# Scaling of the output gates moved from GpSimd to ScalarE, head by head, in a gated delta-rule block

## What is computed

```python
o = gated_delta_rule(q, k, v, g, beta)          # 32 heads, DK = 48, DV = 96
gate = (h @ Wg).reshape(b, t, H, DV)
o = rmsnorm(o, gnorm_w) * jax.nn.silu(gate)
o = o.reshape(b, t, VD) @ Wo
```

## Time and profile before

| | |
|---|---|
| time, median of 3 runs | 2520.83 us |
| lowest, highest | 2520.28, 2522.46 us |
| profiled execution, its own time | 2518.24 us |
| its span, first to last instruction | 2516.3 us |
| mean granted clock of TensorE | 0.978 of 2.4 GHz |
| busy: TensorE, VectorE | 2352.5 us (93%), 2004.9 us (80%) |
| busy: ScalarE, GpSimd | 1407.4 us (56%), 1279.2 us (51%) |

### The profile page before, as it was taken

One profiled execution on the slowest core, in us unless ns is written; L12 is line 12 of the kernel. 1 busy time (PEld: TensorE's weight loads), 2 busy tenths in 40 slices (PEclk: granted clock), 3 DMA queues, 4 the chain that ended last, 5 costly groups with the idle time before them and its releaser, 6 DMA issues. The chain is left out here.

```text
span 2516.3 us, 53535 instructions
## 1 busy us (share of the span) xinstructions
PE 2352.5 (93%) x18800; PEld 1889.7 (75%) x18800; DVE 2004.9 (80%) x4146; ACT 1407.4 (56%) x3331; POOL 1279.2 (51%) x2046
## 2 busy tenths in 40 slices
PE   6599999999999999999999999999999998699997
PEld 2378888888888888888888888888888887546665
DVE  5678888888888888888888888888888887235544
ACT  3256666666666666666666666666666665322221
POOL 3456566666666666666666666656566665100000
PEclk9689999999999999999999999999999999799998
DMA  4211121112111211121112111211121110221100
GB/s 129 69 36 35 27 61 34 34 33 55 35 36 36 54 37 35 36 54 36 36 36 55 36 36 36 55 36 36 36 55 36 36 26 9 66 62 34 34 9 9
DMA packets 203849, 103.20 MB, mean 41 GB/s; under 512 B 97009, under 2 KB 185018, under 8 KB 203586
## 3 DMA queue, kind: packets, MB, share of 16 engines
q1 hardware_dynamic: 203266, 99.65, 17.0%
q10 hardware_dynamic: 320, 0.13, 0.0%
HBM read 69.89 MB, written 2.54 MB: 29 GB/s over the span
## 5 line engine op out<-in xcount | busy, mean ns | idle before, releaser
L861 DVE SCALAR_TENSOR_TENSOR dr_y<-dr_ps,cw,dr_y 128x255 f32<-128x255 f32 (+2 forms) x1152 | 479.9, 472 | 8.9 <-ACT dr_y L986 8.9
L1125 POOL TENSOR_TENSOR dr_fo<-dr_vo,dr_nhalf 128x4 f32<-128x4 f32 x128 | 156.1, 1219 | 539.5 <-DVE dr_vo L941 539.5
L744 PE MATMUL dr_ps<-dr_w,dr_am 128*128 128x96 f32 x3072 | 418.1, 280 | 3.2 <-ACT dr_w L1038 3.2
L744 PEld LDWEIGHTS dr_ps<-dr_w,dr_am 128*128 128x128 f32 x3072 | 380.3, 193 | 12.1 <-ACT dr_w L1038 3.9
L831 DVE TENSOR_TENSOR dr_w<-dr_ps,mask 128x512 bf16<-128x512 f32 x512 | 350.3, 684 | 31.4 <-PE dr_ps L629 24.6
L986 ACT ACTIVATE dr_y<-dr_ps,cw 128x256 f32<-128x256 f32 x384 | 160.9, 470 | 195.1 <-PE dr_ps L676 195.0
L1038 ACT COPY dr_w<-dr_ps 128x384 f32<-128x384 f32 x384 | 188.8, 492 | 134.8 <-PE dr_ps L744 134.8
L972 ACT CAST dr_tn<-dr_ps 128x512 bf16<-128x512 f32 x384 | 226.3, 589 | 55.7 <-PE dr_ps L644 55.6
L873 DVE TENSOR_TENSOR_SCAN dr_dec<-dr_abc,dr_dg 128x512 f32<-128x512 f32 x128 | 208.4, 1628 | 33.4 <-POOL dr_dg L1091 18.1
L975 ACT CAST dr_tt<-dr_ps 128x512 bf16<-128x512 f32 x384 | 233.5, 608 | 0.0
L650 PE MATMUL dr_ps<-dr_tt,dr_w 128*128 128x128 bf16 x2048 | 197.9, 219 | 20.1 <-DVE dr_w L831 20.1
(11 more groups left out here) (204 smaller groups left out, 5059.9 us busy)
## 6 DMA issues: line engine op xcount, KB each, us to landing
dr_abc<-scr_a SPq DMA_DIRECT2D x64, 512.0 KB, 5.4
dr_qk<-dr_sy SPq DMA_DIRECT2D x384, 48.0 KB, 2.0
dr_bcb<-scr_b SPq DMA_DIRECT2D x128, 64.0 KB, 4.6
dr_c<-dr_b SPq DMA_DIRECT2D x512, 4.0 KB, 1.8
dr_qk<-dr_sy SPq DMA_DIRECT2D x128, 32.0 KB, 1.9
ex_modb<-scr_mod SPq DMA_DIRECT2D x4, 1024.0 KB, 8.1
wv<-in_Wv SPq DMA_DIRECT2D x8, 384.0 KB, 3.5
wo<-in_Wo SPq DMA_DIRECT2D x1, 3072.0 KB, 12.1
```

The lines of the kernel that those rows point to most:

```text
L744: last = pe.matmul(ps[:, bank, h * DV:(h + 1) * DV], wt(h), x[:, h * DV:(h + 1) * DV], start=(start and h == 0), stop=(h == QH - 1), skip_ ...
L861: v.scalar_tensor_tensor(y[:, slot, x:T], ps[:, BANK[n], off:off + T - x], cw[:, t, TAPS - 1 - x:TAPS - x], y[:, slot, x:T], ALU.mult, ALU ...
```

## The change

The root of line 1125 stays on GpSimd. The product of line 1129 is taken away, with its two waits. In its place ScalarE gets a step `scale` at the piece `mean`: it waits for the root and the gates, and then scales the gates of each of the 4 heads with one instruction, which reads the head's factor as a scale for each partition. The semaphore `gf_ok` is now raised four times a chunk, so VectorE's wait in `gated` counts to four times as much.

```diff
             def gated(st, c):
                 it, m = st
-                v.wait_ge(s["gf_ok"], it * CH + c + 1)
+                v.wait_ge(s["gf_ok"], (it * CH + c + 1) * QH)
                 v.tensor_tensor(og[:, c], ps[:, CO, 0:QV], gs[:, m, c], ALU.mult).then_inc(s["og_ok"], 1)
...
+            def scale(st, c):
+                it, m = st
+                act.wait_ge(s["fo_ok"], it * CH + c + 1)
+                act.wait_ge(s["gs_ok"], it * CH + c + 1)
+                for h in range(QH):
+                    part = gs[:, m, c, h * DV:(h + 1) * DV]
+                    act.activation(part, part, ACT.Copy, scale=fo[:, h:h + 1]).then_inc(s["gf_ok"], 1)
+
...
-                      w0=w0, delta=delta, state_out=lambda st: squares(st, 0), out=squares, ks=ks, oT=turn_out)
+                      w0=w0, delta=delta, state_out=lambda st: squares(st, 0), out=squares, ks=ks, mean=scale, oT=turn_out)
...
                 pool.tensor_tensor(fo[:], vo[:], nhalf[:], ALU.pow).then_inc(s["fo_ok"], 1)
-                wait(pool, s["gs_ok"], it * CH + c + 1)
-                wait(pool, s["fo_ok"], it * CH + c + 1)
-                heads = gs[:, m, c].rearrange("p (h d) -> p h d", h=QH)
-                pool.tensor_tensor(heads, heads, bc(fo[:], 2, DV), ALU.mult).then_inc(s["gf_ok"], 1)
```

## The result

The changed kernel takes 3087.4 us (median of 4 runs, 3086.64 to 3089.11), the kernel before 2520.9 us: a ratio of 1.2247, 95% interval 1.2226 to 1.2268. It is 566.5 us slower, 8.85 us for each of the 64 iterations.

What follows compares the result with a forecast made beforehand. TensorE was taken to set the turn's length. 5.6 us a turn of idle time plus 4.0 for the lowered clock made 9.6, times 64 is 614 us on 2518.24: 3130 us, range 2870 to 3290.

Steps and rivals of the forecast that it cites:

- Place A: Chunk 0, ScalarE between second negation and cast of line 1058: waiting for the root delays TensorE's solve 3.96 us, net 3.7.
- Place B: Chunk 1, ScalarE between cast of line 975 and copy to `w`: TensorE's residual 2.4 to 2.5 us later, net 2.1.
- What comes back: TensorE regains 0.3 us at line 629, 0.34 before line 727 and 0.2 before line 650, each turn.
- The sum at full clock: Whole turn with TensorE at 2.4 GHz: 3.7 + 2.1 - 0.2 = 5.6 us a turn.
- The clock: TensorE after both idle times: stretches at 1.2 GHz cost 4.0 us a turn, ends 0 and 6.7.
- a mean clock near 0.8: Sign in the kernel's middle: turns of 41 us with this mean clock if the clock does not hold.
- Clock unharmed: Rival for TensorE: clock stays at 2.4 GHz, 5.6 us a turn, 2876 us; chance 0.15.
- Only A lowers it: Rival: only the 3.8 us idle time of chunk 0 brings a low stretch, 7.6 us a turn, 3005 us; chance 0.2.
- Every stretch long: Rival: every low-clock stretch is long and on packed work, 12.3 us a turn, 3305 us; chance 0.1.
- ScalarE has the time: Rival: with the root ready, ScalarE's idle time covers the scalings at both places; 0.13 us a turn, 2520 us; chance 0.03.
- ScalarE's list lets the cast and the copy run ahead: Rival on ScalarE: cast and copy run before the scaling, so no change, 2518 us; chance 0.02.

Runs made afterwards that it cites:

- experiment 7: The changed kernel with GpSimd's selections moved behind the root of chunk 0, so that this root comes first: 2791.0 us, ratio 1.1074.
- experiments 1: The kernel before, plus only a wait on ScalarE for the root at both places, with root and product kept on GpSimd: 2876.5 us, ratio 1.1405.
- experiment 8: The kernel before plus four spare scalings on ScalarE, without a wait, for chunk 0 only: 2520.6 us, ratio 0.9996.
- experiment 5: The changed kernel with filler matmuls that nobody reads, 52 and 30, ahead of TensorE's two waits: 2857.9 us, ratio 1.134.
- experiment 4: The changed kernel with only chunk 1 scaled on ScalarE, chunk 0's product back on GpSimd: 2764.9 us, ratio 1.0963.
- experiment 2: The kernel before plus four scalings of a spare tile on ScalarE at both places, with no wait: 2607.8 us, ratio 1.0331.
- experiment 6: The changed kernel with ScalarE's scaling in a slot of its own, behind later copies to `w`: 2529.5 us, ratio 1.0041.
- experiment 9: The kernel before plus four spare scalings at both places without a wait, and 14 unread matmuls in TensorE's 0.78 us gap: 2542.7 us, ratio 1.0088.
- experiments 3: The changed kernel with only chunk 0 scaled on ScalarE, chunk 1's product back on GpSimd: 2867.7 us, ratio 1.137.

## Why the prediction was right

The forecast was 3130 us, 9.6 us a turn, in a range of 2870 to 3290; measured were 3087.4 and 8.85.

The mechanism was right, and the time came out close partly by luck, since errors in the clock's term offset each other.

- **Place A**, forecast 3.96 us of delay of TensorE's solve: 3.93 us of idle time before it. That it decides there when the root ends, behind the selections, is shown by experiment 7, and that the wait and not the scaling is the main part by experiments 1 and 8. The step of four scalings was mis-sized: the cast began 1.08 us after the first scaling, where the prediction had 0.92. One takes 359 ns (median):

```profile
L1061 ACT ACTIVATE dr_gs<-dr_gs,dr_fo x512: 357/359/376, 166.6 to 2751.8; 128x96 f32<-128x96 f32 x171
```

  By the figures of the Trainium skill, "ScalarE: Activation LUTs", section "What ACT_TABLE_LOAD costs", four were estimated at 1.07 us. The trace agrees with 1.08, and the interpolation from the 128-column row was low. The error was mostly offset by the hand-over from GpSimd, which took 0.03 us where 0.14 was assumed (root to 1601.35, scaling at 1601.38).
- **Place B**, forecast 2.4 to 2.5: 2.31, from a root of 1.01 us, the same hand-over of 0.03 and the same 1.08.
- **What comes back**, forecast 0.8 us a turn (0.3 at A, 0.34 at B, 0.2 before line 650): TensorE's two waits are 6.24 us a turn, and the idle part of the loss is 5.57, so 0.67. The first two came as forecast: line 629 follows line 744 after 0.17 us, and TensorE's wait before its scores is gone in the list of waits. The third did not: the 0.29 us before line 650 stand unchanged.
- **The sum at full clock**, forecast 5.6 us a turn: 5.57 by busy times, 5.3 by the run with the filler.
- **The clock**, forecast 4.0: 3.28 by TensorE's busy time, 3.6 by the run with the filler. Both stalls bring it. This term was right in kind and a tenth to a fifth too large, and that it came so close was luck: the two thirds were chosen, not read. Low stretches of 5.9 us were assumed, of which some fail to come; they come behind every idle time, but are 4.1 us long on average. And the sign "a mean clock near 0.8" did not follow from the term itself: 4.0 us lost at half speed are 8 us at the lower level, which in 41 us is 0.90, as measured.
- **The rivals.** Clock unharmed (2876): refuted by the profile, and its number was nearly met by the run with the filler (2858). Only A lowers it (3005): refuted by experiment 4. The Trainium skill's "TensorE: Matmul & The Clock Gate", section "HAM oscillation — how this bites in real kernels", warns of longer idle gaps only. Here 2.31 us at B brought the low clock, and 0.78 us behind the norms were enough (experiment 2), so the measurement decides against it. Every stretch long (3305): not met. ScalarE has the time: false for where the change put the scaling, since the root is not ready there. With nothing to wait for, A costs nothing, as this rival said (experiment 8; by its own numbers the cast ends at 1247.15 and not at 1247.4, which changes nothing). B costs the 86 us of experiment 2 and not 8, because the rival left out the clock. With a slot of its own the scaling costs 8 us (experiment 6). ScalarE's list lets the cast and the copy run ahead: refuted, both begin behind the fourth scaling in the timeline.

## What to carry to other kernels

Work that is moved to an engine with free time takes its wait along, and everything behind that wait in the engine's list waits too. So read when the input is ready, and what stands next in the list, before reading how busy the engine is; here the same work cost 566 us at one place in the list and 8 us at another, four entries further down at A and one at B. Where TensorE is the bound, as here, price each new idle time twice, once for itself and once for the clock after it.

## What the runs showed of the hardware

- A gap of 0.78 us on TensorE, right behind the twelve matmuls of the norms (8 columns each, 1.47 us together), was followed by the lower clock, 1.2 GHz, in 13 of some 18 turns of experiment 2, and cost 64 us in all. I had expected nothing from a gap of this size. With 14 more matmuls in that gap the clock stayed at 1.00 (experiment 9).
- The length of a gap alone does not decide it. With fillers ahead of them, gaps of 0.94 us at A and 0.62 us at B (at 1251.83 and 1272.92 in experiment 5) left the clock at 1.00, and in the kernel before so did idle times of 0.3 us, and one of 1.05 us near the end of the stage, after which the clock is 1.00 from 2126 to 2136:

```profile
2125.88 1.13 PE L744 MATMUL dr_ps<-dr_w,dr_am 128*128 128x96 f32 x8 [1.05 <-ACT dr_w L1038]
```

- After an idle time of 3.93 us the clock fell too, but this costs no more than after 2.31: 115 against 126 us (experiments 3 and 4).
- VectorE's scan takes 1.22 us at 1587.39 in the changed kernel, where GpSimd works beside it only in its last 0.4 us, and took 1.99 in the earlier trace rows, where GpSimd made the gate gains and the start of `base` beside it. GpSimd's copy in `base` (line 1135, now 1139) took 1167 ns (median of 64) before and takes 236 after; the one at 1584.78 has no work of VectorE beside it. In both kernels a short operation of GpSimd that falls into the other scan of a turn ends about when the scan does: 1.06 us at 1241.54 before (0.27 in the turn of the changed kernel, outside a scan), 1.11 us at 1592.49 after. That the two engines hold each other up is my reading; no run isolates it.
- Why the kernel of experiment 6 is 8 us slower than the one before was not settled. Its trace is of the fastest of its five executions (2523.4 us, mean clock 0.979), with TensorE's busy time the same 2352.5 us; the slower ones (up to 2534.0 us) have mean clocks of 0.971 to 0.977.
